# A decoder layer with attention, int8 experts and a routed feed-forward: a 97th contraction row, fp32r masks, one product for several heads, folds side by side, a new table of turns, and the queries' low parts requested from ScalarE's queue

## What is computed

```python
x = x + attention(layernorm(x))   # 16 heads of 32 for q, one head of k and v; causal softmax; out projection
x = x + xattn(layernorm(x), w, d) # two SmoothQuant int8 linears with silu(gate) * up between
x = x + ffn(layernorm(x))         # 512 -> 1376 -> 512, silu gate, a shared LoRA and 8 routed LoRA experts, top 2
```

## Time and profile before

| | |
|---|---|
| median of three runs | 995.62 us (990.35 to 1001.97) |
| the profiled execution | 999.05 us, its span 997.3 us |
| mean granted TensorE clock | 0.962 |
| TensorE busy | 938.5 us (94% of the span), 5362 matmuls |
| VectorE busy | 614.4 us (62%) |
| ScalarE and GpSimd busy | 315.5 and 310.1 us |
| chain that ended last, share by engine | PE 81%, DVE 6%, ACT 3%, DMA 3%, issue 3% |

### The profile page before, as it was taken

How to read it: one execution, slowest core, us unless ns; L and a number is a source line. 1 busy time by engine, 2 the same in 40 slices (tenths; PEclk the granted TensorE clock), 3 DMA queues, 4 the chain that set the end, 5 groups by cost and what they waited for, 6 DMA issues and landing times.

```text
span 997.3 us, 13830 instructions
## 1 busy us (share of the span) xinstructions
PE 938.5 (94%) x5362; PEld 672.2 (67%) x5370; DVE 614.4 (62%) x945; ACT 315.5 (32%) x544; POOL 310.1 (31%) x393
## 2 busy tenths in 40 slices
PE   6899998689999899999999899999989999899997
PEld 5665576445567676766687666766668787578885
DVE  2375668778876596766756785765567665332222
ACT  2323532345453116253332234334221521120110
POOL 3634631444770132235400141255114023011110
PEclk9887999698799999999999999999999999999999
DMA  8796625343790933358346533372524455535442
GB/s 288 254 313 236 246 106 131 110 129 131 277 337 18 257 107 114 139 209 300 128 156 152 177 121 123 134 276 99 204 74 185 153 192 206 190 126 193 173 162 90
DMA packets 42917, 174.96 MB, mean 175 GB/s; under 512 B 5404, under 2 KB 8220, under 8 KB 32868
## 3 DMA queue, kind: packets, MB, share of 16 engines
q1 hardware_dynamic: 36804, 119.02, 35.2%
q10 hardware_dynamic: 6048, 55.05, 15.3%
HBM read 127.46 MB, written 33.75 MB: 162 GB/s over the span
## 4 chain that ended last, share of the span: by engine, by line
PE 81%; DVE 6%; issue 3%; ACT 3%; DMA 3%; SPq 2%; POOL 1%; POOLq 0%; DVEq 0%
PE ring L984 12%; PE ring L985 12%; PE ring L986 12%; PE ring L981 5%; PE slots L1056 4%; PE av L1088 4%; PE slots L1074 4%; PE ring L1220 4%; PE den L1088 3%; PE slots L984 3%; PE slots L986 3%; PE slots L985 3%; SPq L608 2%; PE slots L1157 2%; PE slots L1053 2%
## 5 line engine op out<-in xcount | busy, mean ns | idle before, releaser
L776 POOL TENSOR_TENSOR hd_l<-hd,hd_h 128x512 fp32r<-128x512 f32 x44 | 57.3, 1302 | 287.7 <-ACT hd_h L951 287.7
L984 PE MATMUL ring<-xT_h,gu 128*128 128x512 f32 x352 | 143.2, 407 | 0.4 <-DVE gated L1544 0.3
L1338 DVE TENSOR_REDUCE negm<-slots 128x1 f32<-128x384 f32 (+3 forms) x176 | 107.2, 636 | 58.2 <-PE slots L1056 57.2
L985 PE MATMUL ring<-xT_l,gu 128*128 128x512 f32 x352 | 137.6, 391 | 0.0
L986 PE MATMUL ring<-xT_h,gu 128*128 128x512 f32 x352 | 137.5, 391 | 0.0
L853 ACT ACTIVATE probs<-slots 128x512 f32<-128x512 f32 (+1 forms) x176 | 90.7, 556 | 97.4 <-PE slots L1074 97.0
L743 POOL TENSOR_SCALAR_AFFINE_SELECT probs<-probs 128x128 f32<-128x128 f32 (+2 forms) x176 | 67.3, 394 | 125.6 <-ACT probs L853 124.8
L1056 PE MATMUL slots<-kst,qst 96*128 96x128 f32 (+3 forms) x256 | 87.2, 416 | 0.0
L1074 PE MATMUL slots<-qst,kst 98*128 98x128 f32 (+3 forms) x256 | 68.5, 357 | 13.2 <-DMA qst<-negm_hl 12.1
L984 PEld LDWEIGHTS ring<-xT_h,gu 128*128 128x128 f32 x352 | 66.3, 188 | 19.6 <-issue 7.1
L986 PEld LDWEIGHTS ring<-xT_h,gu 128*128 128x128 f32 x352 | 66.1, 188 | 14.6
(11 more groups left out here) (195 smaller groups left out, 1807.8 us busy)
## 6 DMA issues: line engine op xcount, KB each, us to landing
gu<-gu_parts ACTq DMA_DIRECT2D x42, 1280.0 KB, 5.5
dn<-dn_parts SPq DMA_DIRECT2D x12, 1728.0 KB, 7.3
...
```

The lines of the kernel that those rows point to most:

```text
L776: pool.tensor_tensor(hd_l[:, i, :], hd[:, i, :], hd_h[:, i, :].bitcast(F32), ALU.subtract).then_inc(hd_lo.sem, 1)
L984: pe.matmul(out_, w_hi_, m_hi_, start=start, stop=False, skip_group_check=True)
L985: pe.matmul(out_, w_hi_, m_lo_, start=False, stop=False, skip_group_check=True)
L1338: dve.tensor_reduce(negm[:, h0:h0 + heads, qt], slot("max", b, g, i)[:, 0, 0:heads * n].rearrange("p (h n) -> p h n", n=n), AX.X, ALU.max, ...
```

## The change

Seven things are changed.

1. `MROW = KROWS + 1 = 97`: a 97th row goes between the scores' 96 and the two rows of maxima. In `kst` it is zero, in `qst` it is a piece of the identity, so it adds nothing. `maxima` multiplies 97 rows, `scores` 99, and the maxima's rows move to 97 and 98.
2. The mask's operands are fp32r (`mask_r`); the identity of the fills and of the bf16 transposes stays bf16 (`ident_bf`). The fills read one 128-column tile twice.
3. `scores` is one matmul a unit, over all its heads, with the same columns in all.
4. `prep_gu` alternates between the gate's and the up side's products.
5. SyncE makes 2 requests for the 97th row ahead of its wait for `q_hi`, and 8 for the high parts, without waiting for `q_lo`.
6. ScalarE makes the 4 requests for the low parts: of the first pair in `q` after `e == 2`, of the second in `v`, each behind a wait for `q_lo` (and for `w_lo`, `wo_lo` or `o_ps`, as SyncE has it).
7. `TURNS` is another table. It has 439 fills where it had 428, 204 of them single (96 before).

```diff
+MROW = KROWS + 1
 TURNS = (
-    "A1A111114111111111114111111414111AA4444111111111111194111141AA1114A14AAAAA1AAA1W41WWAAWAX14XX11X1114X1XXX41XXW"
...
+    "A11A111411111411111111111AA111111111111111141111111111111111111114111111111111111111111111AA11A11AA11AAA111111"
...
-        mask_bf = sb("mask_bf", [P, 2, P], BF16)
+        ident_bf, mask_r = sb("ident_bf", [P, 1, P], BF16), sb("mask_r", [P, 2, P], F32R)
...
+                for g in (2 * ep, 2 * ep + 1):
+                    sp.dma_start(qst[KROWS:MROW, 4 * g:4 * g + 4, :].bitcast(F32), mask_r[0:4 * TT, 0, :].bitcast(F32)).then_inc(q_moved[ep].sem, 16)
+                qst_by_quadrant = qst[:, :, :].rearrange("p (e j) t -> p e j t", j=4)
                 sp.wait_ge(q_hi.sem, q_hi.at(b, e + 1))
-                sp.wait_ge(q_lo.sem, q_lo.at(b, e + 1))
-                qst_by_quadrant = qst[:, :, :].rearrange("p (e j) t -> p e j t", j=4)
-                for j in range(4):
-                    for src, row in ((qT_h, 0), (qT_l, HD), (qT_h, 2 * HD)):
+                for row in (0, 2 * HD):
+                    for j in range(4):
                         sp.dma_start(qst_by_quadrant[row:row + HD, 2 * ep:2 * ep + 2, j, :].bitcast(F32),
-                                     src[HD * j:HD * j + HD, 2 * ep:2 * ep + 2, :].bitcast(F32)).then_inc(q_moved[ep].sem, 16)
+                                     qT_h[HD * j:HD * j + HD, 2 * ep:2 * ep + 2, :].bitcast(F32)).then_inc(q_moved[ep].sem, 16)
...
+                if e == 2:
+                    low_rows(b, 0)
+
+            def v_(b):
+                low_rows(b, 1)
+
+            def low_rows(b, ep):
+
+                if b == 0 and ep == 0:
+                    act.wait_ge(w_lo.sem, KT)
+                elif b == 0:
+                    act.wait_ge(wo_lo.sem, KT)
+                elif ep == 0:
+                    act.wait_ge(o_ps.sem, o_ps.at(b - 1, 2))
+                act.wait_ge(q_lo.sem, q_lo.at(b, 2 * ep + 2))
+                by_quadrant = qst[:, :, :].rearrange("p (e j) t -> p e j t", j=4)
+                for j in range(4):
+                    act.dma_start(by_quadrant[HD:2 * HD, 2 * ep:2 * ep + 2, j, :].bitcast(F32),
+                                  qT_l[HD * j:HD * j + HD, 2 * ep:2 * ep + 2, :].bitcast(F32)).then_inc(q_moved[ep].sem, 16)
...
-                for side in range(2):
-                    rank_rows = slice(32 * side, 32 * side + RANK)
-                    ps = in_ring.claim(pe, ("prep_gu", f, side), folded_gu, 2 * f + side + 1)
-                    for k in range(KT):
-                        mm = pe.matmul(ps[:, k * P:(k + 1) * P], fold[rank_rows, k * P:(k + 1) * P],
+                ps = [in_ring.claim(pe, ("prep_gu", f, side), folded_gu, 2 * f + side + 1) for side in range(2)]
+                for k in range(KT):
+                    for side in range(2):
+                        rank_rows = slice(32 * side, 32 * side + RANK)
+                        mm = pe.matmul(ps[side][:, k * P:(k + 1) * P], fold[rank_rows, k * P:(k + 1) * P],
                                        fold[rank_rows, D + f * P:D + (f + 1) * P], start=True, stop=True, skip_group_check=True)
-                    mm.then_inc(fold_gu_ps.sem, 1)
+                        if k == KT - 1:
+                            mm.then_inc(fold_gu_ps.sem, 1)
...
-                pe.matmul(diagonal, mask_bf[:, 0, :], mask_bf[:, 1:2, :].to_broadcast([P, heads, P]), start=True, stop=False,
+                pe.matmul(diagonal, mask_r[:, 0, :], mask_r[:, 1:2, :].to_broadcast([P, heads, P]), start=True, stop=False,
...
-                for h in range(heads):
-                    mm = pe.matmul(ps[:, 0, h * n:(h + 1) * n], kst[0:KROWS + 2, kt * P:(kt + 1) * P],
-                                   qst[0:KROWS + 2, 4 * g + h0 + h, kt * P:T], start=True, stop=True, skip_group_check=True)
-                mm.then_inc(t_ps.sem, 1)
+                pe.matmul(ps[:, 0, 0:heads * n].rearrange("p (h n) -> p h n", n=n), kst[0:MROW + 2, kt * P:(kt + 1) * P],
+                          qst[0:MROW + 2, 4 * g + h0:4 * g + h0 + heads, kt * P:T], start=True, stop=True, skip_group_check=True)\
+                    .then_inc(t_ps.sem, 1)
```

60 lines of the change are left out of this document (31 added, 29 removed).

## The result

The changed kernel is slower: 1005.51 us median of 20 executions (1000.22 to 1016.18) against 1003.48 of 20 of the kernel before; the ratio is 1.0084, 95% interval 1.0055 to 1.0114. The ratios here compare the fast executions of both kernels, those within 1.5% of the kernel's fastest, which is why this one is larger than the 0.2% between the two medians. 970 us were forecast, in a range of 950 to 988. The profiled execution took 1012.85 us.

The account below looks back on a forecast made before the run. TensorE bounds the kernel after 295 us, TensorE and VectorE together before, with half-clock stretches there. 7.0 us late plus 0.6 of 36 us early (21.6) off 999.05 us gave 970 us, range 950 to 988.

Parts of the forecast that it names:

- The table: New order of turns: fewer fills after the first gate step, 2.6 us, and 3 us off sequence 1's scores wait.
- fills counted at 0.106 us: 25 fewer fills after the first gate step give 2.6 us; 56 more ahead of it lie in TensorE's waits.
- 3 of the 8.86 us wait: Sequence 1's first scores wait 8.86 us for the maxima's two rows; the new order takes off 3.
- Rival C: Slower: the clock drops behind short waits after 295 us that fewer fills bridge; 1010 us with 12 more stretches; chance 0.05.
- The clock, -17 us: Half-clock stretches before 295 us cost TensorE 33 us; shorter or filled waits and denser folds bring back half, 17 us.
- Masks, -1.8 us: Mask products in fp32r: 0.01 us off each of 176 units, 1.8 us, half of it after 295 us.
- the other bound, 7 us: Masks cost 7 us if 0.04 us of the slower f32 weight load shows in each unit.
- Folds, 0.7 us each: Gate and up products in turn run side by side over row groups: 0.7 us, 7.7 us for 11 tiles before 278 us.
- Scores: One product for four heads saves 0.27 us in each of 16 units: 2.2 us in sequences 0 and 1, 2.2 in 2 and 3.
- Requests, 2.6 us a pair: Query requests split over SyncE and ScalarE: 2.6 us each for sequences 0 and 1, 1.3 us for 2 and 3 together.
- The 97th row: Maxima of 97 rows cost nothing in duration; what the row may do is to the clock.
- Rival A: Early stages are held by other engines, VectorE above all, so faster products become waits: 983 us; chance 0.17.

Follow-up runs that it names:

- e1: The changed kernel with the old table of turns, every other edit kept; 0.9906 of the kernel before, 988.21 us.
- e3: The kernel before with two edits alone, one scores product a unit and the two sides of a fold in turn; 0.9928 of the kernel before.
- e18: The changed kernel with the old table and bf16 masks; 0.9907 of the kernel before.
- e12: The changed kernel with the old table, bf16 masks and all query requests on SyncE's queue, the 97th row kept; 0.9890 of the kernel before.
- e9: The changed kernel with the old table up to sequence 0's first gate step, the new one behind it; 0.9983 of the kernel before.

## Why the prediction was wrong

**The table: the step that failed.** I priced the new order by two things, fills counted at 0.106 us (2.6 us less behind gate 0, the extra ones ahead of it free) and 3 of the 8.86 us wait. At 0.6 for the wait that is 4.4 us of gain. It cost 17 to 21 us instead (0.9906 to 1.0084, 1 to 1.0210). That is 22 of the 37 us between forecast and result; the other 15 are the other edits, 9.4 us of gain (0.9906) for 24.2 forecast. Ahead of gate 0 the wait did go, all of it, but into fills and work at a low clock: from kv 1 to those scores e1 has 25.1 us of work and 12.5 of idle time, the changed kernel 30.6 and 4.6, and the stretch is 0.7 us shorter. Behind gate 0 I counted 25 fewer fills as a gain and didn't look at what else the order moved in the stretch with TensorE busy for 97% of the time: there it made 5.5 us of waits more than the old order has, one of them (GpSimd's bias ahead of the cut) to be read in the order of steps before any run.

**Rival C had the outcome and got 0.05; its mechanism is a small part.** The clock does fall where it didn't in the profile before, in the changed kernel at 351.0, 490.9 and 753.7 us, 3.4 us each, behind waits of 2.00, 2.46 and 1.82 us. That is 5 us in this trace. But kernels with the old table have 3.4 to 9.2 us of low clock behind gate 0 too, so at most a few us of it are the table's. The larger part of the loss I hadn't as a rival at all: over all executions 5 us more of clock than e1 in total, and 13 us that aren't clock, of which the traces account for half.

**The clock, -17 us (10 at 0.6).** With the old table it came about: low clock up to gate 0 fell from 69.2 us to between 42.5 and 53.1 in the profiles of e1, e3, e18 and e12 (19.4 and 33.7 us there) and to 60.2 in e9's, and over all executions from 86 us in the whole program to 62 in e1, which is 12 us of time. But it wasn't the 97th row that did this (e3 has none). The new order took back less than half of it in the mean (72 us), though all of it in the profiled execution (82.0 us up to gate 0). I took half of the stretches for gone since "nothing says all go"; nothing said half either.

**Masks, -1.8 us:** +5 us by the units. I took the value from the units that follow a long product; it was the other bound, 7 us, that lay near, 0.03 us in the mean unit and 0.09 behind a bf16 fill. The Trainium skill (the same page, Weight-path perf modes) spoke against this edit, and the traces agree with it in the sign of the sum; between long fp32 products the fp32r mask is the quicker one, 0.286 for 0.300 us.

**Folds, 0.7 us each:** 0.55, so 6.0 us for 7.7. The overlap that the Trainium skill tells of (the same page, Packing small matmuls), which I had read as a full halving, is there in part. **Scores:** 0.27 us a unit of four heads, as forecast. **Requests, 2.6 us a pair:** 0.5 to 1.2, where in sequence 1 requests on two queues at once were slower each (0.91 us for 0.64), and a loss of 2.8 in sequence 3, from a wait in ScalarE's stream that I had named as covered "by that idle time". (The twelve of the earlier trace rows end at 169.3 us; 169.98 is the end of the next pair's first.) **The 97th row:** nothing in duration, as said, and nothing on the clock.

**The sum's form held in part.** With the old table 13.2 us are gone by gate 0 in e1's profile (7.0 in e9's) for the 20 or so that these terms made at 0.6. But of the 4.4 us behind it (without the fills) none arrived: work fell by 1.3 us in e1, and 6.2 us of low clock and 0.8 of idle time came. Rival A's picture, VectorE as the bound, isn't borne out: it is busy for 105.68 of 130 us, and TensorE gained where the order let it. The chances under 986 us add up to 0.85, not 0.84.
